# Graph attention layer on one core: a reordered first stage, two of eight masks of each later block on ScalarE, the queries' low parts on GpSimd

## What is computed

```python
h = relu(layernorm(x)); hs = layer_norm(h); ht = layer_norm(h_target)
q = (ht @ Wq + bq) / sqrt(32); k = hs @ Wk + bk; v = hs @ Wv + bv      # per head
logits = where(adj != 0, q @ k.T, -1e30); probs = softmax(logits)
ht = ht + (probs @ v) @ Wo + bo
ht = layer_norm(ht); ff = gelu(ht @ W1) @ W2
return x + ht + ff
```

## Time and profile before

| what | value |
|---|---|
| runs of before | 689.97, 692.81 and 692.80 us; median 692.8 us |
| the profiled execution | 694.41 us, of it a span of 692.6 us |
| busy in the span | PE 657.6 us (95%), DVE 569.2 us (82%), POOL 524.2 us (76%), ACT 484.0 us (70%) |
| mean granted clock of TensorE | 0.993 |
| main loop, first context matmul to last context_out | 72.0 to 593.5 us |

### The profile page before, as it was taken

The page is one execution under the profiler, slowest core; times in us unless marked ns, Lnnn a source line. Parts: engine busy times, 40 slices in busy tenths (PEclk is TensorE's granted clock), DMA queues, the critical chain, the costliest instruction groups (busy, mean ns, idle before and its releaser), DMA issues. The chain is left out here.

```text
span 692.6 us, 20346 instructions
## 1 busy us (share of the span) xinstructions
PE 657.6 (95%) x8346; PEld 473.0 (68%) x8346; DVE 569.2 (82%) x946; ACT 484.0 (70%) x932; POOL 524.2 (76%) x488
## 2 busy tenths in 40 slices
PE   4898999999999999999999999999999899899998
PEld 4465667766776777677767766777777567557767
DVE  5987899989999879999997798989868888575661
ACT  4865668766778858677787686778866788867550
POOL 3574889889999957899998678999977777471430
PEclk9998999999999999999999999999999999999999
DMA  8735501113001011220011112012000000000001
GB/s 296 258 80 153 177 31 36 59 63 108 2 2 34 2 62 63 58 82 2 2 33 33 62 33 78 17 51 74 2 2 2 2 3 2 1 1 32 24 17 54
DMA packets 20797, 36.23 MB, mean 52 GB/s; under 512 B 2752, under 2 KB 13280, under 8 KB 20704
## 3 DMA queue, kind: packets, MB, share of 16 engines
q1 hardware_dynamic: 20704, 34.92, 16.2%
HBM read 26.49 MB, written 2.10 MB: 41 GB/s over the span
## 5 line engine op out<-in xcount | busy, mean ns | idle before, releaser
L1412 POOL TENSOR_TENSOR prob_lo<-prob 128x512 f16<-128x512 f32 x382 | 437.1, 1169 | 74.1 <-ACT prob L888 73.2
L888 ACT ACTIVATE prob<-score 128x512 f32<-128x512 f32 x512 | 304.1, 597 | 135.8 <-PE score L469 128.3
L469 PE MATMUL score<-nidentb,mask_nat 128*128 128x128 bf16 x2048 | 199.1, 220 | 4.1 <-ACT qT L905 1.9
L469 PE MATMUL early<-kT,qT 96*128 96x512 f16 x512 | 192.9, 382 | 10.5 <-DVE half_max L1203 10.1
L469 PEld LDWEIGHTS ctx<-v_sb,prob 128*128 128x128 bf16 x2048 | 159.0, 98 | 60.2 <-ACT raw L910 12.6
L469 PE MATMUL score<-qT,kT 97*128 97x512 f16 x512 | 196.3, 383 | 0.0
L1203 DVE CUSTOM_DVE_ANT_0 early<-early,mask_nat,half_max 128x1024 f32<-128x1024 f32 x128 | 163.6, 1287 | 38.0 <-PE early L469 36.0
L469 PE MATMUL ctx<-v_sb,prob 128*128 128x65 f16 x2048 | 191.4, 193 | 2.3 <-ACT raw L910 1.8
L469 PE MATMUL ctx<-v_sb,prob_lo 128*128 128x65 f16 x2048 | 190.4, 193 | 0.0
L469 PEld LDWEIGHTS ctx<-v_sb,prob_lo 128*128 128x128 f16 x2048 | 142.6, 97 | 49.9 <-issue 4.0
L1203 DVE CUSTOM_DVE_ANT_0 early<-early,mask_nat 128x1024 f32<-128x1024 f32 x128 | 157.1, 1229 | 22.5 <-PE early L469 20.8
(11 more groups left out here) (167 smaller groups left out, 623.2 us busy)
## 6 DMA issues: line engine op xcount, KB each, us to landing
adj_in<-in_adj SPq DMA_DIRECT2D x26, 512.0 KB, 4.0
qT<-q_stage SPq DMA_DIRECT2D x48, 64.0 KB, 2.0
kT<-mask_nat SPq DMA_DIRECT2D x48, 64.0 KB, 2.0
raw<-in_x SPq DMA_DIRECT2D x4, 512.0 KB, 5.6
tgt<-in_L_gnn_h_target SPq DMA_DIRECT2D x4, 512.0 KB, 11.6
prob<-in_adj SPq DMA_DIRECT2D x4, 512.0 KB, 10.4
nT<-in_L_gnn_W SPq DMA_DIRECT2D x2, 1024.0 KB, 6.6
mask_nat<-in_x SPq DMA_DIRECT2D x1, 2048.0 KB, 8.3
```

Of the source, the lines that this page charges most:

```text
L469: return nc.tensor.matmul(dst, w, m, start=start, stop=stop, **more)
L888: nc.scalar.activation(prob[:, n % SLOTS, :], score[n % 2][:, :], ACT.Exp).then_inc(exp_done, 1)
L1412: nc.gpsimd.tensor_tensor(prob_lo[:, n % SLOTS, :], prob[:, n % SLOTS, :], prob_hi(n % SLOTS), ALU.subtract).then_inc(lo_sem["pool"], 1)
```

## The change

Masks of the later blocks: those numbered 1 to 6 stay on DVE at the places they had. Masks 0 and 7, which DVE made at (1,0) and (5,3), go to ACT, each in four parts of 128 x 512: two squares of the integer edges, written as float32 over `adj_in`, and two rectified lines, relu(1e30 - 1e30 * square), into the mask. Their steps lie at (0,2), (0,4), (0,11), (0,13) for mask 0 (in block 0 at (1,2), (1,4), (1,6), (1,8)) and at (5,13), (5,15), (6,1), (6,3) for mask 7. Queries: ACT now copies the biased product to `cT` in float32 (`query_out`, at the old step, frees `aux`), takes the high part from there one step later, and POOL subtracts at (4,8) and (5,2). The first stage is put in another order on all four engines, with 24 more unread matmuls.

```diff
+UNREAD_LATER = 24
-MASK_DVE = [(1, 0), (2, 3), (2, 6), (3, 2), (3, 7), (4, 3), (4, 7), (5, 3)]
+MASK_DVE = {(2, 3): 1, (2, 6): 2, (3, 2): 3, (3, 7): 4, (4, 3): 5, (4, 7): 6}
+MASK_ACT = {0: [(0, 2), (0, 4), (0, 11), (0, 13)], 7: [(5, 13), (5, 15), (6, 1), (6, 3)]}
+MASK_ACT_0 = [(1, 2), (1, 4), (1, 6), (1, 8)]
+        q_full, q_low_at = cT, [(4, 8), (5, 2)]
...
 (SP, before place_q)
-                            sp.wait_ge(aux_done, AUX["qp", k + 1, 1] + 1)
+                            sp.wait_ge(q_hi, DC * (k + 1))
+                            sp.wait_ge(q_lo, DC * (k + 1))
...
 (PE, first stage)
                 project(1)
                 turn_rows(2)
                 values(0)
+                for i in range(UNREAD_LATER):
+                    mm(early[1][:, TB:TB + P], identb[:, :], identb[:, :], True, True)
+                project(2, (0,))
                 turn_rows(3)
-                project(2)
+                project(2, (1,))
                 values(1)
+                project(3, (0,))
                 turn_rows(4)
-                project(3)
-                values(2)
-                for i in range(2):
-                    early_scores(0, i)
-                project(4)
-                for e in range(1, RAMP + 2):
+                project(3, (1,))
+                for e in range(2):
                     for i in range(2):
                         early_scores(e, i)
-                    if e + 2 < NT // 2:
-                        values(e + 2)
-                shift_row(0)
+                project(4)
+                for e in range(2, RAMP + 2):
+                    if e == RAMP + 1:
+                        shift_row(0)
+                    for i in range(2):
+                        early_scores(e, i)
+                    if e < NT // 2:
+                        values(e)
...
 (ACT)
+                def mask_part(k, i, part):
+                    edges = adj_home(k, i)[:, part % 2 * TB:(part % 2 + 1) * TB]
+                    squares = edges.bitcast(F32)
+                    done = 2 * (masks_act(k, i) - 1)
+                    if part < 2:
+                        if part == 0:
+                            slot, use = adj_use(k, i)
+                            act.wait_ge(adj_here[slot], 16 * use)
+                            if i == 0:
+                                masks_free(act, k)
+                        nc.scalar.activation(squares, edges, ACT.Square).then_inc(edges_sq, 1)
+                    else:
+                        act.wait_ge(edges_sq, done + part - 1)
+                        last = nc.scalar.activation(mask_half(k, i)[:, part % 2 * TB:(part % 2 + 1) * TB], squares, ACT.Relu,
+                                                    bias=big_c, scale=-BIG)
...
                 def query_high(k, m):
+                    act.wait_ge(aux_done, AUX["qp", k, m] + 1)
+                    nc.scalar.activation(q_stage[:, 0, m, :], q_full[:, m, :], ACT.Copy).then_inc(q_hi, 1)
+
+                def query_out(k, m):
                     job_here("qp", k, m)
-                    nc.scalar.activation(q_stage[:, 0, m, :], aux[:, :], ACT.Identity, bias=Q_B[:, m:m + 1]).then_inc(q_hi, 1)
+                    nc.scalar.activation(q_full[:, m, :], aux[:, :], ACT.Identity, bias=Q_B[:, m:m + 1]).then_inc(aux_done, 1)
...
 (ACT, first stage: features(2) goes ahead of deviation(2) and high_parts(1); last_sources behind high_parts(2);
  high_parts(4) ahead of the target deviations and the table of Exp; high_values(7) behind row_out(0))
...
 (DVE, first stage: low_parts(0) ahead of second_scale(2); masks 0 to 3 around low_parts(2); target_stats(1) and (2)
  go from ahead of the masks to behind maxima(3) and maxima(4))
...
-                def query_low(k, m):
-                    dve.wait_ge(q_hi, DC * (k - 1) + m + 1)
-                    nc.vector.scalar_tensor_tensor(out=q_stage[:, 1, m, :], in0=aux[:, :], scalar=Q_B[:, m:m + 1],
-                                                   in1=q_stage[:, 0, m, :], op0=ALU.add, op1=ALU.subtract).then_inc(aux_done, 1)
...
 (POOL)
+                def query_low(k, m):
+                    pool.wait_ge(q_hi, DC * (k - 1) + m + 1)
+                    nc.gpsimd.tensor_tensor(q_stage[:, 1, m, :], q_full[:, m, :], q_stage[:, 0, m, :], ALU.subtract).then_inc(q_lo, 1)
...
                 source_norm(1)
+                drop_sources(1)
                 source_norm(2)
-                drop_sources(1)
                 drop_sources(2)
```

More of the change, by code:

```diff
@@ L161, in masks_dve, with masks_act, act_mask_at @@
 def masks_dve(k, i):
-    return min(i + 1, FIRST_DVE) if k == 0 else PAIRS * (k - 1) + FIRST_DVE + i + 1
+    return min(i + 1, FIRST_DVE) if k == 0 else len(MASK_DVE) * (k - 1) + FIRST_DVE + min(i, len(MASK_DVE))
+def masks_act(k, i):
+    return len(MASK_ACT) * (k - 1) + 1 + (i == PAIRS - 1) if k > 0 else 0
+def act_mask_at(k, r, s):
+    for i, steps in MASK_ACT.items():
+        if k == 0 and i == 0:
+            steps = MASK_ACT_0
+        if (r, s) in steps:
+            return i, steps.index((r, s))
+    return None
 def gnn_kernel(nc, x, adj, nodemask, h_target, ln1_scale, ln1_bias, Wq, bq, Wk, bk, Wv, bv, Wo, bo,
@@ L346, in mask_ready @@
             eng.wait_ge(mask_dve, masks_dve(k, h * TT + TT - 1))
+            if k > 0:
+                eng.wait_ge(mask_act, masks_act(k, h * TT + TT - 1))
             if k == 0 and h == 1:
@@ L484, in turn_rows, with project @@
                         last.then_inc(tp_ready, 1)
-                def project(g):
+                def project(g, halves=range(DC)):
                     what = GROUPS[g]
@@ L495, in project @@
                         pe.wait_ge(bc_done, 1)
-                    for m in range(DC):
+                    for m in halves:
                         if g == 0 and m == 1:
@@ L1010, in _ @@
                 high_parts(3)
+                high_parts(4)
+                high_values(2)
+                feature_sum(0)
+                feature_sum(1)
+                for i in range(3, 6):
+                    high_values(i)
                 for k in range(1, 3):
@@ L1188, in make_mask @@
                     dve.wait_ge(adj_here[slot], 16 * use)
-                    if k > 0 and i == 0:
+                    if k > 0 and i == 1:
                         masks_free(dve, k)
@@ L1286, in _ @@
                 second_scale(3)
-                low_parts(0)
                 low_parts(1)
                 low_values(0)
+                make_mask(0, 0)
+                low_parts(2)
+                for i in range(1, TT):
+                    make_mask(0, i)
+                low_values(1)
+                low_parts(3)
+                maxima(0)
+                maxima(1)
+                low_parts(4)
+                maxima(2)
+                low_values(2)
+                make_mask(0, 4)
+                maxima(3)
+                make_mask(0, 5)
                 target_stats(1)
-                low_parts(2)
+                maxima(4)
                 target_stats(2)
-                low_values(1)
-                for i in range(2):
-                    make_mask(0, i)
-                low_parts(3)
-                for i in range(2, TT):
-                    make_mask(0, i)
-                maxima(0)
-                low_values(2)
-                low_parts(4)
-                maxima(1)
-                make_mask(0, 4)
-                maxima(2)
-                make_mask(0, 5)
-                for e in range(3, RAMP + 1):
+                for e in range(5, RAMP + 2):
                     maxima(e)
-                for e in range(RAMP + 1, RAMP + FILL):
+                for e in range(RAMP + 2, RAMP + FILL):
                     maxima(e)
@@ L1317, in _ @@
                                 normed_low(0, HT_AT[r, s - 2])
-                            if k + 1 < NTB and (r, s - 3) in QP_AT:
-                                query_low(k + 1, QP_AT[r, s - 3])
                         for n in lo_here(u, j):
@@ L1490, in _ @@
                             context_sum(k - 1, SUM_AT.index((r, m)))
+                        if k + 1 < NTB and (r, m) in q_low_at:
+                            query_low(k + 1, q_low_at.index((r, m)))
                         if m == 12 and u in LOW_AT:
```

44 lines of the change are left out of this document (26 added, 18 removed).

## The result

The changed kernel takes 687.62 us, the median of 6 runs (687.53 to 688.57); the kernel before takes 692.8 us (6 runs, 689.97 to 693.06). The ratio is 0.9936, with a 95% interval of 0.9919 to 0.9953: 0.64% faster. The forecast was 685.0 us, 1.1% less, with a range of 681.0 to 690.8 us. The sign and the range held, and the gain was two thirds of what I had said. The kernel before ran 77 times more beside the experiments, with medians of 691.4 to 691.7 us; against those the gain is 3.8 to 4.1 us, about half of what I had said. One execution of all, the profiled one of the kernel with the masks back on VectorE, took 2373 us and is left aside. The profiled executions stand 6.85 us apart (694.41 and 687.56 us; spans 692.6 and 685.8 us).

A forecast was written before the change was run, and what follows sets the result against it. TensorE, busy 95% of the span, was taken as the bound, leaving its waits, half-clock stretches and the first stage. Terms -3.8 -1.4 -1.6 -1.5 -2.8 +2.5 +0.4 +0.4 = -7.8 us gave 685.0 us from 692.8, range 681.0 to 690.8.

The forecast's parts named there:

- (k,1) and (0,1): Step 6, TensorE waits for a maximum behind mask 0 on VectorE: 0.8 us off in blocks 1 and 2, 1.4 in block 0.
- rival 5: Squares on ScalarE force table loads, 31 us there, a third hidden: 705 us; chance 0.03.
- Rival 3: ScalarE has no room: 24 mask parts and 6 copies cost TensorE 0.25 us each, 692.5 us; chance 0.09.
- The unit's end: Mask 7's square at (5,15) delays context_out: 0.4 us per unit, counted only in block 2, +0.4 us.
- (k,4): Step 10, blocks 1 and 2: query_low leaving VectorE removes 0.75 of a 0.85 us wait for a maximum, -1.5 us.
- (k,5): Unit 0.93 us above a quiet one; query_low and mask of (5,3) leaving VectorE remove all, three times: -2.8 us.
- GpSimd: +2.5 forecast: Query subtractions make GpSimd late at (k+1,0): TensorE waits 1.1 us in blocks 0 and 1, 0.3 in block 2.
- Rival 4: GpSimd's new operations stretch VectorE's low parts where VectorE is late, 6 x 0.5 = 3 us: 688.0 us; chance 0.06.
- First stage: Before the loop: maximum earlier 2.3 us, shift row 0.7, clock 0.8; 3.8 us less in all, bounds 1.0 to 6.
- step (iv): First stage, 62.68 to 69.06 us at half clock: 0.8 us of up to 2.3 us taken as gain.
- (ii): First stage, half-clock projection of 3.65 us: unread matmuls and the earlier start fill the idle time ahead, 1.7 us more.
- the three terms: Bounds given: first stage -1.0 to -6, (0,1) 0 to -1.4, GpSimd 1.5 to 4 us.

The follow-up runs named there:

- the kernel with both edits and the queries on VectorE: Changed kernel with mask 7's ScalarE parts at (6,1), (6,2), (6,4), (6,5), the scale at pair 6, and queries' parts as in the kernel before: 689.16 us.

## Why the prediction was right and where not

- **(k,1) and (0,1): right.** -0.81, -0.81 and -1.44 us against -0.8, -0.8 and -1.4. These prices came from a comparison of two units, one with the mask and one without, and from a wait at the very place.
- **ScalarE's parts: right in price.** In the changed kernel, against the earlier trace rows:

```profile
L1015 ACT ACTIVATE mask_nat<-adj_in,big 128x512 bf16<-128x512 f32 x12 | 8.6, 716 | 0.0
L1012 ACT ACTIVATE adj_in<-adj_in 128x512 f32<-128x512 int32 x12 | 7.5, 622 | 0.0
L1022 ACT ACTIVATE q_stage<-cT 128x512 f16<-128x512 f32 x6 | 3.9, 643 | 0.0
```

  622 and 716 ns (columns: line, engine, operation, shapes, count, busy us, mean ns, idle before) against 630 and 690, and no table load for the square: rival 5 is out. Rival 3 is out too: the kernel with the masks alone gains 1.9 us.
- **The unit's end: the size per unit was right, the count not.** The last step of (k,5) is 0.41 us longer (0.4 forecast), but in all three blocks; I had let two of them fall into a wait for GpSimd that did not exist. (0,11) and (0,13) cost 0.19 us in each of two units, against 0.4 in all. Not forecast: the extra copy at (4,14) costs the end of each (k,4) 0.16 us.
- **(k,4): the step that failed.** The prediction said that `query_low` is "0.75 of 0.85 us" there. It stood in time in which VectorE would have idled; the wait belonged to the two small operations of the scale behind it and to the low part that follows. In the kernel before the first of the two took 0.90 us, the second 0.17 and the low part 1.54; in the changed kernel 0.98, 0.97 and 0.68. From the reciprocal to the next maximum both need 2.7 us, so the delay only changed its member; with the scale moved away the low part takes 0.74 us there and the wait is gone. I had named the scalings in the queue and priced the wrong member. Moving them alone gave 2.6 us. The (k,4) units were to lose 1.5 us and are 0.59 us longer, summed over the blocks: 2.1 of the 2.4 us by which the loop fell short; the rest is mostly 0.17 us in (2,7). That comes with the masks (15.08 us with the masks only, 14.91 with the queries only); its cause stays open.
- **(k,5): the same error.** The gain of 2.8 us did not come; the three units together are 0.24 us longer, the square included. The mask of (5,3) did give 0.28 us in each block, and the square took it back. `query_low` was again ahead of an idle spell: in the changed kernel the maximum behind it waits for TensorE. Moving it to GpSimd gave 0.22 us in (1,5) and (2,5) and cost 0.20 in (0,5) (15.99 us against 15.77 and 16.19). The 0.44 us at step 3 are mask 6, as its move showed.
- **GpSimd: +2.5 forecast.** In (1,5) one weight load waits 0.3 us for a low part, and the waits of TensorE's matmuls for GpSimd sum to 0.5 us in the span, as before:

```profile
L498 PE MATMUL ctx<-v_sb,prob 128*128 128x65 f16 x2048 | 191.5, 193 | 3.1 <-ACT raw L944 2.6 <-POOL prob_lo L1472 0.5
L1277 DVE TENSOR_TENSOR prob_lo<-prob 128x512 f16<-128x512 f32 x130 | 134.3, 1034 | 4.1 <-ACT prob L922 4.0
L1517 POOL TENSOR_TENSOR q_stage<-cT,q_stage 128x512 f16<-128x512 f32 x6 | 7.0, 1158 | 1.7 <-ACT q_stage L1022 1.6
```

  The term rested on TensorE being 0.93 us early at (k,5). Without that gain there was nothing to give back: the two terms were one error and nearly cancelled. With the unit's end they said -2.8 + 2.5 + 0.4 = +0.1 us, and +0.24 came. GpSimd did take up its idle time, none is left in (1,5). Its weight part beside the removed mask went from 1.60 to 1.15 us, the 0.45 that I had allowed.
- **Rival 4** was real and hidden: VectorE's 130 low parts went from a mean of 984 to 1034 ns, 6.5 us in all (1010 ns with the queries alone, 1018 with the masks alone, so the queries are only a part of it). Where VectorE has no slack, with all masks on it, (k,5) is 2.0 us longer in the three blocks together, of the 2.5 us that the queries cost; the room that the masks leave pays for it. It should have been a term of the sum, tied to the masks, and not a case beside it.
- **First stage: mechanism half right, size off.** The projection started at 29.09 and took 1.94 us, and the eighth maximum ended at 59.9 us (60.3 forecast, 62.6 before). I gave the clock 0.8 us in step (iv) and the order the rest of 3.8; the runs give the order 0.8 and the clock 4.4 in the profiled pair. The unread matmuls, to which I gave part of it in (ii), do nothing that the runs can tell.
- **The carry to the median was wrong in kind.** I took 7.8 us from 694.41 and then from 692.8. A change that ends half-clock stretches takes more from an execution that had many than from the median one: 6.85 us there, 5.2 us between the medians. That is 1.7 of the 2.6 us by which 685.0 was too low; the other 0.95 us is the sum's own error, 2.4 us too much in the loop less 1.4 too little in the first stage.
- **The bounds.** Added up, the stated bounds of the three terms give 681.8 to 690.7 us, not 681.5 to 689.5. The range of 681.0 to 690.8 us covers both.

## What to carry to other kernels

Before a wait is put down to the operation ahead of it on the queue, ask whether that operation itself stood in idle time: take it away in thought and see who waits then. Ahead of a wait the small operations count as well, for beside a busy neighbour with whom they share a path they may cost as much as the large ones. Two edits that use and make room on the same engine should be priced as four combinations. And where one program's executions scatter in steps, sort them by the granted clock before any median is explained.

## What the runs showed of the hardware

- A VectorE operation on 4 elements per row with two SBUF inputs takes 0.16 us beside an idle GpSimd and 0.98 us beside a busy one: about as much longer, 0.8 us, as a low part of 512 elements (0.76 and 1.51 us). A reciprocal of 8 elements, with one input, takes 0.20 us in both.
- After a wait of TensorE of 1.89 us (in the loop) and 3.34 us (in the first stage) the granted clock was 0.50; in the loop, after waits of 1.39, 1.08 and 0.88 us, it stayed at 1.00. In the first stage of the kernel before, waits of 1.19 and 1.15 us were followed by 0.50 in the profiled execution, while the same code with waits of 1.19 and 1.16 us kept 1.00 in another. The times of the kernel with both edits and the queries on VectorE lie 1.6 to 1.7 us apart, step by step, as its mean clock goes from 1.0 to 0.998 and 0.995.
- So the same code behind the same waits gets either level: from 30 to 35 us it was granted 0.67 in one execution and 1.00 in another. What decides between them these runs don't show.
- A square of int32 to float32, 128x512, takes 622 ns on ScalarE, a rectified line with a pointer bias to bf16 716 ns, between exponentials and without a table load.
